# DLRM interaction tower: 13 one-hot features in rounds of two, 13 gathered features a tile

## What is computed

```python
    def _L0_rec_ref(dense_proj, sparse_embs):
        ...
        all_vecs = jnp.concatenate([dense_proj[:, None, :], sparse_embs], axis=1)
        interactions = jnp.einsum('bnd,bmd->bnm', all_vecs, all_vecs)
        interact_flat = interactions[:, rows, cols]
        return jnp.concatenate([dense_proj, interact_flat], axis=1)
    ...
    h = jnp.concatenate([z, r_dense_proj], axis=1)
    h = jnp.maximum(h @ W_top1 + b_top1, 0.0)
    h = jnp.maximum(h @ W_top2 + b_top2, 0.0)
    y = h @ W_top3
```

## Time and profile before

| what | us |
|---|---|
| runs | 147.99, 144.15, 147.20 |
| median | 147.2 |
| the profiled execution, whole time | 143.05 |
| its span, first to last instruction | 141.2 |
| TensorE, VectorE, ScalarE, GpSimd busy | 100.0, 79.5, 46.3, 69.1 |
| moved by DMA | 15.22 MB |

### The profile page before, as it was taken

One profiled execution on the slowest core, in us unless ns is written; L12 is line 12 of the kernel. 1 busy time (PEld: TensorE's weight loads), 2 busy tenths in 40 slices (PEclk: granted clock), 3 DMA queues, 4 the chain that ended last, 5 costly groups with the idle time before them and its releaser, 6 DMA issues.

```text
span 141.2 us, 3356 instructions
## 1 busy us (share of the span) xinstructions
PE 100.0 (71%) x1384; PEld 74.6 (53%) x1384; DVE 79.5 (56%) x190; ACT 46.3 (33%) x75; POOL 69.1 (49%) x68
## 2 busy tenths in 40 slices
PE   0079999999989989973432121177999995995880
PEld 0067876887758665751311010085687784684460
DVE  5399799999999999988000000048065177014101
ACT  3123649787665636740000000022132221040220
POOL 4787878888888778778787777200000000000000
PEclk9999999999999999996555555559999999999999
DMA  2899999997989999321222112100000000000000
GB/s 78 236 244 255 233 238 240 208 247 240 202 189 245 320 219 312 111 58 39 56 60 56 50 43 56 37 0 5 5 5 5 5 0 0 5 5 5 0 0 1
DMA packets 7337, 15.22 MB, mean 108 GB/s; under 512 B 2045, under 2 KB 2686, under 8 KB 7322
## 3 DMA queue, kind: packets, MB, share of 16 engines
q1 hardware_dynamic: 5402, 11.07, 31.1%
q0 software_dynamic: 1920, 3.94, 11.4%
HBM read 14.99 MB, written 0.00 MB: 106 GB/s over the span
## 4 chain that ended last, share of the span: by engine, by line
PE 41%; issue 24%; POOL 23%; DMA 6%; DVE 2%; ACT 1%; DVEq 0%
POOL gathered L316 23%; PE gram_ps L522 12%; PE l_ps L573 6%; DMA gathered<-in_tbl,ids_sb 5%; PE fill_ps L492 4%; PE fill_ps L494 3%; PE fill_ps L508 3%; PE l_ps L545 3%; PE l_ps L549 2%; PE l_ps L552 2%; PE l_ps L548 2%; PE turn_ps L560 2%; DVE by_sample L453 1%; PE turn_ps L532 1%; DMA ids_sb<-in_ids 1%
## 5 line engine op out<-in xcount | busy, mean ns | idle before, releaser
L316 POOL DMA_INDIRECT gathered<-in_tbl,ids_sb x60 | 68.3, 1138 | 19.2 <-issue 18.0
L492 PE MATMUL fill_ps<-hot,tab_hi 125*128 125x512 f32 x92 | 39.0, 424 | 8.5 <-DVE tab_lo L413 7.9
L405 DVE TENSOR_SCALAR hot<-ids_bc,row_id 125x512 fp32r<-125x512 int32 x92 | 40.2, 480 | 1.8 <-DMA ids_bc<-in_ids_t 1.8
L494 PE MATMUL fill_ps<-hot,tab_lo 125*128 125x512 f32 x92 | 37.4, 407 | 0.0
L522 PE MATMUL gram_ps<-vec 128*32 128x27 f32 x1024 | 18.6, 204 | 23.9 <-issue 23.9
L522 PEld LDWEIGHTS gram_ps<-vec 128*32 128x32 f32 x1024 | 14.4, 120 | 30.1 <-issue 30.1
L492 PEld LDWEIGHTS fill_ps<-hot,tab_hi 125*128 125x128 f32 x92 | 18.2, 198 | 15.6 <-issue 11.6
L446 DVE COPY_PREDICATED pairs<-second,gram_ps 128x104 f32<-128x104 int32 x16 | 4.4, 272 | 38.2 <-issue 22.6
L494 PEld LDWEIGHTS fill_ps<-hot,tab_lo 125*128 125x128 f32 x92 | 18.3, 199 | 3.3
L413 DVE TENSOR_TENSOR tab_lo<-tab_raw,tab_hi 125x256 fp32r<-125x256 f32 (+1 forms) x44 | 18.9, 429 | 1.6 <-ACT tab_hi L333 1.4
L333 ACT CAST tab_hi<-tab_raw 125x512 fp32r<-125x512 f32 (+1 forms) x22 | 14.3, 660 | 14.9 <-DMA tab_raw<-in_tbl 14.2
(11 more groups left out here) (46 smaller groups left out, 58.6 us busy)
## 6 DMA issues: line engine op xcount, KB each, us to landing
tab_raw<-in_tbl SPq DMA_DIRECT2D x8, 448.0 KB
ids_bc<-in_ids_t SPq DMA_DIRECT2D x11, 256.0 KB
tab_raw<-in_tbl SPq DMA_DIRECT2D x2, 560.0 KB
gathered<-in_tbl,ids_sb POOLq DMA_INDIRECT x60
w_raw<-in_w_pairs SPq DMA_DIRECT2D x3, 256.0 KB
w_sb<-in_W_top SPq DMA_DIRECT2D x1, 512.0 KB
tab_raw<-in_tbl SPq DMA_DIRECT2D x2, 224.0 KB
tab_raw<-in_tbl SPq DMA_DIRECT2D x8, 52.0 KB
```

The costliest lines, as they stand in the source:

```text
L316: pool.indirect_dma_start(out=gathered[:, n % GSLOTS, j, :], out_offset=None, in_=tables[f], in_offset=bass.IndirectOffsetOnAxis(ap=ids_sb ...
L405: nc.vector.tensor_scalar(hot[0:HP, n % HOTS, :], ids_bc[0:HP, o % TSLOTS, :], row_id[0:HP, j:j + 1], None, ALU.is_equal).then_inc(hot_mad ...
L492: nc.tensor.matmul(into, tab_hi[0:HP, c % HALVES, cols], hot[0:HP, n % HOTS, :], start=(j == 0), stop=False)
L494: used = nc.tensor.matmul(into, tab_lo[0:HP, c % HALVES, cols], hot[0:HP, n % HOTS, :], start=False, stop=(j == NK[o] - 1))
```

## The change

Features 5 and 12 (1,250 rows) move from the gathered to the one-hot way: 13 of each, so 52 gathers in batches of four, three, three and three, in six slots instead of eight. The one-hot features now go in seven rounds: feature 2 alone, then six pairs. One compare makes the one-hot columns of a chunk for both features of a round (1,024 columns), one subtraction makes both `tab_lo` parts, and one cast makes two chunks of both features (a piece). Three pieces are kept of `tab_hi`, `tab_lo` and `hot`; tables and ids are kept for three rounds. Inside a piece TensorE does feature after feature, into two banks. There are four fill banks; the layer-2 result, which had a bank of its own, takes the fourth after the one-hot part, and batches then go on with three. In the list, tile 0's Gram units stand after `hot(6)`, `batch(2, 1)` and `batch(2, 2)`.

```diff
-ONEHOT = [2, 3, 6, 7, 8, 19, 21, 23, 25, 0, 4]
-NK = [8] * 9 + [10] * 2
+ROUNDS = [[2], [3, 6], [7, 8], [19, 21], [23, 25], [0, 4], [5, 12]]
+NK = [8, 8, 8, 8, 8, 10, 10]
+NR = len(ROUNDS)
+WIDE = 2
+ONEHOT = [f for fs in ROUNDS for f in fs]
+FIRST_OF = [sum(len(fs) for fs in ROUNDS[:r]) for r in range(NR)]
 NH = len(ONEHOT)
 MAXK = max(NK)
 GATHERED = [f for f in range(FEATURES) if f not in ONEHOT]
 
-BATCHES = [GATHERED[i:i + 4] for i in range(0, len(GATHERED), 4)]
+BATCHES = [GATHERED[0:4], GATHERED[4:7], GATHERED[7:10], GATHERED[10:13]]
 NB = len(BATCHES)
 MAXB = max(len(b) for b in BATCHES)
+
+PIECE = 2
+PIECES = [(r, i) for r in range(NR) for i in range(NK[r] // PIECE)]
 TSLOTS = 3
-HALVES = 3
-HOTS = 12
-GSLOTS = 8
-FBANKS = 3
+PSLOTS = 3
+HOTS = PIECE * PSLOTS
+GSLOTS = 6
+
+FBANKS = 4
...
-    out = hot(0) + hot(1) + [("dense",)] + batch(0, 0) + hot(2) + batch(0, 1) + hot(3) + batch(0, 2)
-    out += hot(4) + batch(0, 3) + hot(5) + batch(1, 0) + hot(6) + batch(1, 1) + hot(7) + hot(8) + batch(1, 2)
-    out += hot(9) + batch(1, 3) + hot(10) + batch(2, 0) + gram(0, 0) + batch(2, 1) + gram(0, 1, 2, 3)
-    out += gram(1, 0) + batch(2, 2) + [("turn", 0)] + gram(1, 1) + [("l1", 0)] + gram(1, 2) + [("h1t", 0)]
-    out += batch(2, 3) + gram(1, 3) + [("l2", 0)] + gram(2, 0) + [("turn", 1)] + batch(3, 0) + gram(2, 1)
+    def hot(r):
+        return [("hot", r)]
+
+    out = hot(0) + [("dense",)] + hot(1) + batch(0, 0) + batch(0, 1) + hot(2) + batch(0, 2) + batch(0, 3)
+    out += hot(3) + batch(1, 0) + batch(1, 1) + hot(4) + batch(1, 2) + hot(5) + batch(1, 3) + batch(2, 0)
+    out += hot(6) + batch(2, 1) + batch(2, 2) + gram(0, 0, 1, 2, 3)
+    out += gram(1, 0) + batch(2, 3) + [("turn", 0)] + gram(1, 1) + [("l1", 0)] + gram(1, 2) + [("h1t", 0)]
+    out += gram(1, 3) + [("l2", 0)] + gram(2, 0) + [("turn", 1)] + batch(3, 0) + gram(2, 1)
     out += [("l1", 1)] + gram(2, 2) + [("h1t", 1)] + batch(3, 1) + gram(2, 3) + [("l2", 1)] + batch(3, 2)
...
+L2_BANK = FBANKS - 1
+BANK_OF = [i % FBANKS if i <= FILL_OF["fill", NH - 1] else (i - FILL_OF["fill", NH - 1]) % (FBANKS - 1)
+           for i in range(len(FILLS))]
+
+FORMER = [max([j for j in range(i) if BANK_OF[j] == BANK_OF[i]], default=None) for i in range(len(FILLS))]
+LAST_IN_L2 = max(i for i in range(len(FILLS)) if BANK_OF[i] == L2_BANK)
...
-        tab_raw = sb("tab_raw", [P, TSLOTS, MAXK * D], F32)
-        ids_bc = sb("ids_bc", [P, TSLOTS, TILES * P], I32)
-        tab_hi = sb("tab_hi", [P, HALVES, MAXK // 2 * D], F32R)
-        tab_lo = sb("tab_lo", [P, HALVES, MAXK // 2 * D], F32R)
-        hot = sb("hot", [P, HOTS, TILES * P], F32R)
+        tab_raw = sb("tab_raw", [P, TSLOTS, WIDE, MAXK * D], F32)
+        ids_bc = sb("ids_bc", [P, TSLOTS, WIDE, TILES * P], I32)
+        tab_hi = sb("tab_hi", [P, PSLOTS, WIDE, PIECE * D], F32R)
+        tab_lo = sb("tab_lo", [P, PSLOTS, WIDE, PIECE * D], F32R)
+        hot = sb("hot", [P, HOTS, WIDE, TILES * P], F32R)
...
-        l2_ps = ctx.enter_context(nc.psum_tensor("l2_ps", [P, 512], F32))
         turn_ps = ctx.enter_context(nc.psum_tensor("turn_ps", [P, 4, P], F32))
+
+        l2_out = fill_ps[:, L2_BANK, 0:HID2]
...
+        def wait_piece_used(eng, c):
+
+            r, i = PIECES[c]
+            if i == NK[r] // PIECE - 1:
+                eng.wait_ge(fill_made, FILL_OF["fill", FIRST_OF[r] + len(ROUNDS[r]) - 1] + 1)
             else:
-                eng.wait_ge(hot_used, chunk(o, j) + 1 - o)
-
-        def wait_half_used(eng, c):
-
-            wait_chunk_used(eng, c // 2, chunks_of(c)[-1])
+                eng.wait_ge(piece_used, c + 1 - r)
...
+            def load_tables(r):
+
+                slot = r % TSLOTS
+                if r >= TSLOTS:
+                    sp.wait_ge(hot_made, PIECE * (piece(r - TSLOTS, 0) + NK[r - TSLOTS] // PIECE))
+                for k, f in enumerate(ROUNDS[r]):
+                    sp.dma_start(ids_bc[:, slot, k, :], ins["ids_t"][f:f + 1, :].to_broadcast([P, TILES * P])) \
+                        .then_inc(bc_landed[slot], 16)
+                if r >= TSLOTS:
+                    sp.wait_ge(tab_lo_made, PIECE * (piece(r - TSLOTS, 0) + NK[r - TSLOTS] // PIECE))
+                for k, f in enumerate(ROUNDS[r]):
+                    src = tables[f].rearrange("(p k) d -> p (k d)", p=HP)
+                    halves = [(0, NK[r] * D, table_landed[slot])]
+                    if r == 0:
+                        m = NK[0] // 2 * D
+                        halves = [(0, m, first_half_landed), (m, 2 * m, table_landed[slot])]
+                    for m, n, landed in halves:
+                        for a, b in ((0, 112), (112, HP)):
+                            sp.dma_start(tab_raw[a:b, slot, k, m:n], src[a:b, m:n]).then_inc(landed, 16)
...
-            for o in range(2, NH):
-                load_table(o)
-                if o == NH - 2:
+            for r in range(2, NR):
+                load_tables(r)
+                if r == NR - 2:
...
+            def split_piece(c):
+
+                r, i = PIECES[c]
+                if r == 0 and i == 0:
                     act.wait_ge(first_half_landed, 32)
-                elif c == 1 or c % 2 == 0:
-                    act.wait_ge(table_landed[o % TSLOTS], 32 * (o // TSLOTS + 1))
-                if c >= HALVES:
-                    wait_half_used(act, c - HALVES)
-                n = len(ks) * D
-                nc.scalar.copy(tab_hi[0:HP, c % HALVES, 0:n], tab_raw[0:HP, o % TSLOTS, ks[0] * D:ks[0] * D + n]) \
+                elif i == (NK[r] // PIECE // 2 if r == 0 else 0):
+                    act.wait_ge(table_landed[r % TSLOTS], TABLE_LANDS[r])
+                if c >= PSLOTS:
+                    wait_piece_used(act, c - PSLOTS)
+                n = len(ROUNDS[r])
+                nc.scalar.copy(tab_hi[0:HP, c % PSLOTS, 0:n, :],
+                               tab_raw[0:HP, r % TSLOTS, 0:n, PIECE * D * i:PIECE * D * (i + 1)]) \
                     .then_inc(tab_hi_made, 1)
...
+                if kind == "hot":
+                    r = step[1]
+                    for i in range(NK[r] // PIECE - 1):
+                        if piece(r, i) + PSLOTS < len(PIECES):
+                            split_piece(piece(r, i) + PSLOTS)
+                    for k in range(len(ROUNDS[r])):
+                        copy_fill(FILL_OF["fill", FIRST_OF[r] + k])
+                    if piece(r, NK[r] // PIECE - 1) + PSLOTS < len(PIECES):
+                        split_piece(piece(r, NK[r] // PIECE - 1) + PSLOTS)
+                    if r >= NR - THIRDS:
+                        k = r - (NR - THIRDS)
+                        act.wait_ge(w1_landed[k], 16)
+                        nc.scalar.copy(w1_hi[:, k, :], w1_raw[:, k, :]).then_inc(w1_hi_made, 1)
+                elif step in FILL_OF and not BY_DVE[FILL_OF[step]]:
+                    copy_fill(FILL_OF[step])
...
+            for c, (r, i) in enumerate(PIECES):
+                row_id, n, slot = row_id8 if NK[r] == 8 else row_id10, len(ROUNDS[r]), r % TSLOTS
+                if i == 0:
+                    dve.wait_ge(bc_landed[slot], BC_LANDS[r])
+                if c >= PSLOTS:
+                    wait_piece_used(dve, c - PSLOTS)
+                for k in range(PIECE):
+                    j = PIECE * i + k
+                    nc.vector.tensor_scalar(hot[0:HP, (PIECE * c + k) % HOTS, 0:n, :], ids_bc[0:HP, slot, 0:n, :],
+                                            row_id[0:HP, j:j + 1], None, ALU.is_equal).then_inc(hot_made, 1)
+                    if k == 0:
                         dve.wait_ge(tab_hi_made, c + 1)
-                        if c >= HALVES:
-                            wait_half_used(dve, c - HALVES)
-                    first = js[0] - chunks_of(c)[0]
-                    cols = slice(first * D, (first + len(js)) * D)
-                    nc.vector.tensor_tensor(tab_lo[0:HP, c % HALVES, cols],
-                                            tab_raw[0:HP, o % TSLOTS, js[0] * D:(js[-1] + 1) * D],
-                                            tab_hi[0:HP, c % HALVES, cols].bitcast(F32), ALU.subtract) \
-                        .then_inc(tab_lo_made, 1)
+                    nc.vector.tensor_tensor(tab_lo[0:HP, c % PSLOTS, 0:n, k * D:(k + 1) * D],
+                                            tab_raw[0:HP, slot, 0:n, j * D:(j + 1) * D],
+                                            tab_hi[0:HP, c % PSLOTS, 0:n, k * D:(k + 1) * D].bitcast(F32),
+                                            ALU.subtract).then_inc(tab_lo_made, 1)
...
+                if kind == "hot":
+                    r = step[1]
+                    n, fills = len(ROUNDS[r]), [FILL_OF["fill", FIRST_OF[r] + k] for k in range(len(ROUNDS[r]))]
+                    for i in range(NK[r] // PIECE):
+                        c, last_piece = piece(r, i), i == NK[r] // PIECE - 1
+                        for f in range(n):
+                            if i == 0 and FORMER[fills[f]] is not None:
```

(17 more changed lines are left out.)

132 lines of the change are left out of this document (35 added, 97 removed).

## The result

The changed kernel took 139.37 us, median of 5 runs (138.71 to 141.28), against 147.2 us (142.28 to 149.0) for the kernel before in the same comparison: ratio 0.971, 95% interval 0.964 to 0.977. The medians alone would give 0.947; the ratio is that of each kernel's fast runs (up to 1.5% above its fastest), since both kernels have slower ones, too. It is faster by 3%; I had named 135.5 us, 8% under the median of before. A later set on another chip changes the sign; that stands with e15 and e16. The profiled execution of after took 141.28 us with a span of 139.5.

A forecast was written before the change was run, and what follows sets the result against it. The prediction took GpSimd's gathers to hold TensorE's Gram passes: last gather 79, plus 3.5 us, plus a 49.0 us tail made 131.5 us of span, 133.3 us profiled, named as 135.5 us, range 127 to 145.

The forecast's parts named there:

- tail: TensorE's dense work after the slow Gram passes: 48.7 us of span before, forecast at 49.0 us.
- The step that failed: GpSimd's gathers in the one-hot stage: two would fit in three VectorE cycles of 1.00 us, 1.50 us each.
- two points: A gather was taken to need a shared resource about 0.44 and 0.75 us after its start, open only during VectorE's subtraction.
- stretch only beside compares: The claim that GpSimd's gathers take longer than their 0.94 us alone only while VectorE runs compares.
- rival (b): GpSimd gets no faster: gathers take two whole cycles (2.0 us), hole and tail as before, 143 to 147 us; chance 0.10.
- The hole: TensorE's Gram matmuls crawl in 0.70 us steps while GpSimd gathers; 29.8 us before, forecast to end 3.5 us after the last gather.
- (a): The stretch of slow Gram passes has its own length, 29.8 us from the first Gram unit: 155 us, slower; chance 0.09.
- (c): The stretch of slow Gram passes is gone or short because Gram units start late: 125 us; chance 0.11.
- The wide compare: VectorE's single compare for both features: forecast 0.66 us in a cycle of 1.00 us, against 0.79 us for two narrow ones.
- Rival (d): VectorE's wide compare saves nothing, taking 0.79 us: 134 to 138 us; its chance lies within the forecast's 0.70.
- DMA as the new limit: Loads bound the one-hot stage: VectorE waits some 8 us in all, and Gram units start about 74 instead of 62.7 us.
- Why that costs nothing here: Gram units' 11 us later start lies in the slow stretch; last gather ends about 79 us, TensorE free at 82.5 instead of 92.5.

The follow-up runs named there:

- e15: The changed kernel, unedited, on the chip of set 4: 127.97 us, ratio 1.073 to the kernel before.
- e16: The kernel before, unedited, profiled on the chip of set 4: 119.85 us as the set's reference is listed, its own median 119.13 us.
- e1: Changed kernel plus a one-element memset on VectorE behind each wide subtraction: 141.92 us, ratio 0.966 to the kernel before.
- e9: Changed kernel plus a 64-element memset behind each wide subtraction: 141.24 us, ratio 0.956 to the kernel before.
- e10: Changed kernel plus a 128-element memset behind each wide subtraction: 143.39 us, ratio 0.961 to the kernel before.
- e11: Changed kernel with 14 one-hot features and 48 gathers, plus a 64-element memset in each wide cycle: 138.08 us, ratio 0.935 to the kernel before.
- e12: Changed kernel plus a 288-element memset behind each wide subtraction: 151.16 us, beside 122.56 us for the kernel before.
- e4: Changed kernel plus eight extra gathers behind the last one, into an unused slot (60 gathers): 151.48 us, ratio 1.031 to the kernel before.
- e3: Changed kernel with 16 gathers left out in tiles 2 and 3 (36 gathers): 133.75 us, ratio 0.916 to the kernel before.
- sets 4 and 5: The run sets holding e12 to e16, all on one chip; the kernel before took 122.56 us in set 4 and 119.85 us in set 5.
- sets 1 to 3: The run sets holding e1 to e11, on three other chips; the kernel before took 145.79, 143.93 and 148.69 us there.
- e5: The changed kernel, unedited, as the reference in set 2: 138.33 us, ratio 0.958 to the kernel before.
- e8: Changed kernel with features 2 and 16 as a seventh pair (14 one-hot features, 48 gathers): 135.04 us, ratio 0.934 to the kernel before.
- e6: Changed kernel plus a 64-element subtraction on one partition behind each wide subtraction: 167.67 us, ratio 1.155 to the kernel before.
- e7: Changed kernel plus a 128-element subtraction on one partition behind each wide subtraction: 171.79 us.
- e2: Changed kernel with each wide compare made as two narrow ones: 142.38 us, ratio 0.971 to the kernel before.

## Why the prediction went wrong

Taken against the profile of after, the sum of the forecast comes apart like this: last gather 88.1 instead of 79 (+9.1), free passes 1.9 instead of 3.5 us behind it (-1.6; in the other profiles with slow steps up to the end it is 1.1 to 2.8, so the single 3.46 of before was an extreme), tail 49.5 instead of 49.0 (+0.5). 131.5 + 8.0 is the measured 139.5.

That the median, 139.37, lies only 3.9 us from the 135.5 named and inside the range of 127 to 145 is partly luck. Profile against profile the forecast is 8.0 us off (133.3, measured 141.28). I had added 2.2 us because the runs of before lay above their profiled one; of after the profiled run was the longest of five, 1.9 us above the median.

- **The step that failed** is "Walking the same two points through a cycle that is closed for 0.66 and open for 0.34 us gives two gathers in three cycles, 1.50 us each". The gathers took 2.00 us. Both inputs of the walk were right (0.67 and 0.33), the walk was not: two points fitted to one pattern reproduce that pattern and need not hold in another. By the walk the gather from 40.03 us should have met both needs, at 40.47 and 40.78, in the subtraction's part from 40.48 to 40.82, and taken 0.94 us; it took 1.69. The margin there is 0.04 us, and by the prediction's own inputs it is 0.34 - 0.31 = 0.03, not the 0.09 that it states. Whether a wider margin would have saved it stays open: e1, e9, e10 and e11 did not lengthen the cycle by more than 0.02 us, and in e12 the gathers hung. That gathers "stretch only beside compares" was misread too: the one at 64.69 us of before stretched beside subtractions.
- That makes it rival (b), at 0.10 in my chances. Its spacing and count were right (two whole cycles each, 40 gathers out by 72 us where it said 38, last gather as before); its 143 to 147 us were too high, since it took hole and tail over whole. Of the 9.1 us at the last gather nearly all is the failed step's: 40 gathers instead of 47 at 72 us are seven at 1.25 us, and one of the rest was held for 1.0 us more by the three subtractions. e4 shows the tail following the last gather.
- **The hole** was read rightly for these chips (e3, e4), with (a) and (c) refuted there. That it would be there on every chip was not in the profile. On the chip of sets 4 and 5 the time, 127.97 us, is near the 125 of (c), but the kernel before loses its hole there too, so the change costs 8 us. I had weighed "the hole is gone" only for the changed kernel.
- **The wide compare**: 0.67 of a cycle of 1.00 us, forecast 0.66 and 1.00. Rival (d) falls.
- **DMA as the new limit**: VectorE's stage ended at 70.1 us (forecast 72), the Gram units began at 73.36 (74), after VectorE's waits of 3.4 us until 16.25 us, 1.2 until 22.84 and 1.0 near 61; the forecast had some 8 us, the first of it at 11 to 15. The share of 1.04 in both stretches bears it out. The slots and the four banks cost nothing that the waits show.
- **"Why that costs nothing here"** holds where the passes are slow and only there; e15 and e16 put the price without the cover at 8 us by the medians, 13 by the two profiles.

## What to carry to other kernels

Before moving work behind a stall, ask what the time is where the stall is missing, for the kernel before as well: an uncaused hole may belong to the chip or its state, and a change that only fills it loses there. Where two engines' instructions lock to each other's cycle, a walk through one measured pattern is no price for another cycle: bound the spacing by one, two and more whole cycles, and measure. A filler instruction is no neutral probe; look first whether it lengthened the cycle at all, and then whether the other engine is still let through.

## What the runs showed of the hardware

- Streams of small matmuls beside gathers crawl in 0.7 us steps in the first comparison and on the three chips of sets 1 to 3, and run freely on that of sets 4 and 5, with the same instructions, the same gather times (0.94 us, 1.25 apart) and a DMA share of 0.17 to 0.20 in both. They come free again 1.1 to 3.5 us after the last gather, and during a single gather of 2.3 us or more (e1, e5, e10, e11). The granted clock is at its half level (1.2 GHz) in the crawling stretch, 0.50 from 76 to 86 us before and 1.00 (2.4 GHz) there in e16; the passes were in steps before the clock fell (in e8 from 77.54, the fall at 78.6 us), so the clock did not start it. Nor were instructions still being loaded: in before no packet of an instruction queue moved from 72 to 92 us, while passes came a few at a time. The cause is open: only gathers are shown to matter, and the chip or something that goes with it (one chip without the steps, seen in two sets).
- Gathers can be shut out by VectorE for 15.5 us (e6, cycle of 1.13 us with a subtraction of 64 elements on one partition in it) and 24.7 us (e7, 128 elements, 1.20 us).
- A gather beside three 128x512 subtractions is held until 0.81 to 0.82 us after their end (before, after, e5).
- A memset of 64 or 128 elements in front of the wide compare is nearly free: the compare's own time shrinks by 0.06 and 0.12 us, and the cycle grows by 0.01 and 0.02.
- In the profiles of e1, e2 and e10, VectorE stood idle for 8.2, 9.7 and 7.1 us before 29 to 32 us (in e3 and e4 twice for 2 to 4 us), and the 21st gather waited for TensorE in turn. The first Gram pass came at 79 to 87 us in all five, in e4 too, whose instructions up to there are those of the changed kernel (73.4, 75.3 and 75.1 in its own three profiles). So it comes and goes between executions. In e1 the stall ends at 29.32 us as SyncE's loads run out (its queue takes 73% from 26 to 28 us and 2% from 29 to 30), so VectorE seems to have waited for them; that was not tried.
